# Applying two layernorms of a four-stage transformer kernel on ScalarE instead of VectorE and GpSimd

## What is computed

```python
def _layernorm(x, axis=-1, eps=1e-05):
    m = jnp.mean(x, axis=axis, keepdims=True)
    v = jnp.var(x, axis=axis, keepdims=True)
    return (x - m) / jnp.sqrt(v + eps)
...
    x = _layernorm(x + _L0_attn_ref(x, ...), axis=-1)
    x = _layernorm(x + _L0_ffn_ref(x, ...), axis=-1)     # 32 experts, 6 per token, and a shared one
    x = _layernorm(x + _L1_attn_ref(x, ...), axis=-1)
    x = _layernorm(x + _L1_ffn_ref(x, ...), axis=-1)     # gate/up/down, 384 hidden features
```

## Time and profile before

| | us |
|---|---|
| median of 3 runs | 1186.25 (1186.06 to 1188.51) |
| profiled execution, its own time | 1185.4 |
| span of its trace | 1183.6 |
| TensorE busy | 1059.0 (89%) |
| VectorE busy | 822.5 (69%) |
| ScalarE busy | 763.7 (65%) |
| GpSimd busy | 442.6 (37%) |

### The profile page before, as it was taken

One profiled execution on the slowest core, in us unless ns is written; L12 is line 12 of the kernel. 1 busy time (PEld: TensorE's weight loads), 2 busy tenths in 40 slices (PEclk: granted clock), 3 DMA queues, 4 the chain that ended last, 5 costly groups with the idle time before them and its releaser, 6 DMA issues. The chain is left out here.

```text
span 1183.6 us, 21086 instructions
## 1 busy us (share of the span) xinstructions
PE 1059.0 (89%) x5936; PEld 500.8 (42%) x5936; DVE 822.5 (69%) x1933; ACT 763.7 (65%) x983; POOL 442.6 (37%) x457
## 2 busy tenths in 40 slices
PE   3999999999999965999999999977999999999694
PEld 1122222222222224777778777832333333322573
DVE  4879998999999627887778777846444544422487
ACT  1067777777777873555555555546888888899352
POOL 0312413313211115666667656643333223300264
PEclk9999999999999986999999999978999999999898
DMA  5453222122120001434332443133331233210001
GB/s 162 130 183 95 78 65 94 50 77 81 50 94 15 2 1 34 137 120 133 114 95 92 142 120 114 62 121 107 108 93 62 59 106 106 67 39 2 1 27 45
DMA packets 74073, 97.11 MB, mean 82 GB/s; under 512 B 12700, under 2 KB 42268, under 8 KB 73628
## 3 DMA queue, kind: packets, MB, share of 16 engines
q1 hardware_dynamic: 74024, 96.51, 26.4%
HBM read 68.29 MB, written 27.79 MB: 81 GB/s over the span
## 5 line engine op out<-in xcount | busy, mean ns | idle before, releaser
L577 DVE TENSOR_REDUCE a_nmax<-a_ps_f 128x1 f32<-128x512 f32 x512 | 322.5, 684 | 41.0 <-PE a_ps_f L445 37.5
L390 ACT ACTIVATE a_prob<-a_ps_s 128x1024 f32<-128x1024 f32 x256 | 252.4, 1025 | 77.0 <-PE a_ps_s L505 75.3
L924 ACT ACTIVATE a_prob<-a_ps_s 128x1024 f32<-128x1024 f32 x256 | 249.2, 1033 | 45.4 <-PE a_ps_s L978 42.7
L1763 POOL TENSOR_TENSOR moe_hl<-moe_hid,moe_hh 128x512 fp32r<-128x512 f32 x136 | 176.1, 1299 | 112.3 <-ACT moe_hh L1657 112.2
L445 PE MATMUL a_ps_f<-a_ks,a_qs 48*128 48x512 bf16 x512 | 176.9, 414 | 28.6 <-DMA a_ks<-parts_k 10.3
L1647 ACT ACTIVATE moe_ps<-moe_ps 128x512 f32<-128x512 f32 x128 | 74.5, 582 | 118.2 <-PE moe_ps L1579 117.3
L991 PE MATMUL a_ps_o<-a_prob,a_va 128*32 128x512 f32 x1024 | 138.1, 612 | 2.4 <-ACT a_osb L912 1.3
L518 PE MATMUL a_ps_o<-a_prob,a_va 128*32 128x512 f32 x1024 | 138.0, 612 | 0.3
L445 PEld LDWEIGHTS a_ps_f<-a_ks,a_qs 48*128 48x128 bf16 x512 | 40.2, 94 | 231.2 <-DVE a_nmax L577 190.8
L505 PE MATMUL a_ps_s<-a_qs,a_ks 51*128 51x512 bf16 x512 | 135.1, 387 | 3.2 <-ACT a_prob L390 2.8
L1695 DVE TENSOR_TENSOR moe_prod<-moe_cw,moe_ps 128x512 f32<-128x512 f32 x128 | 87.5, 683 | 61.2 <-PE moe_ps L1579 52.8
(11 more groups left out here) (229 smaller groups left out, 1575.8 us busy)
## 6 DMA issues: line engine op xcount, KB each, us to landing
moe_cw<-r_weights SPq DMA_DIRECT2D x256, 128.0 KB, 2.9
parts_q<-a_parts SPq DMA_DIRECT2D x48, 256.0 KB, 2.5
parts_k<-a_parts SPq DMA_DIRECT2D x48, 256.0 KB, 2.5
a_qs<-parts_q SPq DMA_DIRECT2D x128, 96.0 KB, 2.3
a_ks<-parts_k SPq DMA_DIRECT2D x128, 96.0 KB, 2.4
a_xt<-in_x_t SPq DMA_DIRECT2D x8, 256.0 KB, 2.9
out_x<-g_X SPq DMA_DIRECT2D x8, 256.0 KB, 2.3
moe_wg<-in_wg SPq DMA_DIRECT2D x1, 1088.0 KB, 5.2
```

Of the source, the lines that this page charges most:

```text
L390: nc.scalar.activation(prob[:, u % PSLOTS, :, :], ps_s[:, u % 2, :, :], ACT.Exp, scale=float(P) ** -0.5).then_inc(exp_done, 1)
L577: nc.vector.tensor_reduce(nmax[:, half_no, h % 2, col:col + 1], ps_f[:, bank, :], AX.X, ALU.max, negate=True).then_inc(max_done, 1)
L924: nc.scalar.activation(prob[:, u % PSLOTS, :, :], ps_s[:, u % 2, :, :], ACT.Sigmoid, scale=float(HD) ** -0.5).then_inc(exp_done, 1)
L1763: nc.gpsimd.tensor_tensor(hl[:, part_at(j), :], hid[:, hid_at(j), :], hh[:, part_at(j), :], ALU.subtract).then_inc(hl_done, 1)
```

## The change

The apply of both feed-forward stages moves to ScalarE, as `Identity` with a scale and a bias per token: x * rstd + (-mean * rstd). GpSimd computes that bias in two more small operations right behind `rstd`. The experts' last block stays with GpSimd, with its semaphore count adjusted. Line numbers behind the first edit are 2, then 19 to 21 higher than before.

```diff
@@ layernorm_buffers
-            "rstd": sb("rstd", [P, NT]), "gate": sb("gate", [P, 1]),
+            "rstd": sb("rstd", [P, NT]), "minus": sb("minus", [P, NT]), "bias": sb("shift", [P, NT]),
+            "gate": sb("gate", [P, 1]),
@@ layernorm_apply_pool
-    pool.wait_ge(ln["centred"], b + 1)
+    pool.wait_ge(ln["centred"], 2 * b + 1)
@@
+def layernorm_bias(nc, pool, g, ln, b):
+
+    zero = g["zero"][:, :].broadcast_to([P, NT])
+    nc.gpsimd.tensor_tensor(ln["minus"][:, :], zero, ln["mv"][:, :, 0], ALU.subtract).then_inc(ln["centred"], 1)
+    pool.wait_ge(ln["pool"], 2 * b + 2)
+    pool.wait_ge(ln["centred"], 2 * b + 1)
+    nc.gpsimd.tensor_tensor(ln["bias"][:, :], ln["minus"][:, :], ln["rstd"][:, :], ALU.mult).then_inc(ln["centred"], 1)
+
+
+def layernorm_apply_act(nc, act, g, ln, b, y):
+
+    act.wait_ge(ln["centred"], 2 * b + 2)
+    for k in range(NT):
+        ins = nc.scalar.activation(g["X"][:, b, k, :], y[:, k, :], ACT.Identity, scale=ln["rstd"][:, k:k + 1],
+                                   bias=ln["bias"][:, k:k + 1])
+    ins.then_inc(ln["x_done"], 1)
@@ feed_forward, ScalarE's step
                     head.scalar(act, head_at(b, j))
+                if end_of(b, j, 3) is not None:
+                    layernorm_apply_act(nc, act, g, ln, end_of(b, j, 3), y)
                 if end_of(b, j) is not None:
@@ feed_forward, VectorE's step
-                if end_of(b, j, 3) is not None and not routed:
-                    layernorm_apply(nc, dve, g, ln, end_of(b, j, 3), y)
@@ feed_forward, GpSimd's step
                     layernorm_pool(nc, pool, g, ln, end_of(b, j, 2))
-                if end_of(b, j, 3) is not None and routed:
-                    layernorm_apply_pool(nc, pool, g, ln, end_of(b, j, 3), y)
+                    layernorm_bias(nc, pool, g, ln, end_of(b, j, 2))
```

## The result

The kernel became slower, by more than forecast:

| | before | after |
|---|---|---|
| median of the runs side by side | 1186.15 us (4 runs) | 1231.52 us (4 runs) |
| ratio of the medians, 95% interval | | 1.0382 (1.0357 to 1.0406) |
| profiled execution: time, span | 1185.4, 1183.6 us | 1229.75, 1227.9 us |
| granted clock over the span | 0.970 | 0.956 |

A forecast was written before the change was run, and what follows sets the result against it. It took the experts as bound by TensorE, the last stage by TensorE's 6.7 us a block plus VectorE's apply. 18.7 + 7 + 5.6 = 31.3 on 1185.4 gave 1216.7, stated as 1217 us, range 1199 to 1229.

The forecast's parts named there:

- The wait and its loop: Last stage: ScalarE's apply waits 3.2 us for GpSimd's bias, holding up copy, Silu and high part, in a loop each block.
- The break-even rival: Whole kernel: ScalarE's wait costs what VectorE's stretched apply did, 1186 us; chance 0.01.
- The turn without the clock: Last stage: one block's loop takes 10.5 us in place of 8.06; with the last two layernorms +18.7 us.
- TensorE's clock: Last stage: the clock falls after idle times of 3.8 us; 1 us for each of 7 blocks, +7 us.
- stays low: Rival, last stage: the clock stays low throughout, 3.5 us for each of 7 blocks, 1234 us; chance 0.06.
- The experts: Experts: `hl` reaches TensorE 1.0 us late; 0.8 us for each of 7 blocks, +5.6 us.
- VectorE gains nothing: Both stages: VectorE loses eight applies of 1.1 to 3.1 us from its busy time, and that gains nothing.
- the bias is there in time: Rival, last stage: activations find their bias ready, turns fall to TensorE's 6.7 us, 1181 us; chance 0.04.
- The cheap loop: Rival: the wait stands, but an activation takes 0.30 us and the clock stays up, 1200 us; chance 0.13.

The follow-up runs named there:

- e1: Changed kernel with ScalarE's apply moved to the end of its step, behind the copy, the Silu and the high part: 1191.65 us, 1.0048 to the kernel before.
- e4: Changed kernel with 16 unused 512-column matmuls added on TensorE in each of five last-stage blocks, where it waits for the copy: 1219.47 us, ratio 1.0283.
- e5: Kernel before with the two new small buffers of each layernorm's set laid out and never used: 1189.09 us, ratio 1.0030.
- e9: e8 with GpSimd's old order in the last stage, `hl` ahead of the bias: 1181.41 us, ratio 0.9958 to the kernel before.
- e8: Changed kernel with experts as before; last stage: new buffers, apply behind the high part, bias ahead of `hl`, last two blocks on VectorE: 1178.73 us.
- e6: Changed kernel with GpSimd's `ve`, `rstd` and bias operations ahead of `hl` in the last stage: 1214.10 us, ratio 1.0233 to the kernel before.
- e7: Changed kernel with the apply's activations as plain copies, without scale and bias: 1212.72 us, ratio 1.0221 to the kernel before.
- e2: Changed kernel with the change in the last stage only, the experts normalised on GpSimd as before: 1224.58 us, ratio 1.0326 to the kernel before.

## Why the prediction failed in its size

Point by point, against the profiled executions (44.35 us in all, 31.3 forecast):

- **The wait and its loop: right.** Place, length (3.2 forecast, 3.25), what waits behind it, and TensorE's idle time (3.8 forecast, 3.94) are in the trace. e1 shows that it is the place that costs: 40 of 45 us go with the apply's move alone. The break-even rival needed a turn of 8.1 us; even with a full clock it takes 10.8 (e4).
- **The turn without the clock: 10.5 forecast, 10.8 measured (e4).** Of the 0.3, 0.12 us are the activation, taken as 0.45 and measured at 0.479, four times; the rest is 0.1 each in GpSimd's chain (3.17 us from `hl` to the apply, 3.06 in the sum) and in TensorE's part (4.26 for 4.18). The six turns and the end make 1.9 us, and the last stage at full clock is about 77.2 us where the sum has 75.3: this term was +20.6, not +18.7.
- **TensorE's clock: +7 forecast, some 14 measured. This is the step that failed.** The prediction took 1 us of at most 3.5 a block, because "part of the slow time falls on work off the path". The trace shows the reverse. The clock is at 0.50 from the end of the idle time on, and what TensorE does first then is exactly what the block waits for: 11 of the 15 matmuls of the path, and the turns, run at the low level, and the clock comes up in the twelfth. The last three and the work off the path find it up again. That "the clock comes back in between" was right, but nearly all of the path has then run. The measured cost is 2.7 us a turn (e4).
- **The range.** The working gives the clock up to 3.5 us a block, and that bound alone, with the other terms as they are, is the 1234 us of the "stays low" rival. The range stops at 1229, so it left the step's own bound out. Of the 13 us by which the sum falls short, 6.8 are the clock, 5.0 the experts and 1.9 the turn; the part ahead of the experts gave 0.7 back.
- **"Stays low" as a rival** had the full price and was given 0.06, since the clock does recover in each block. It recovers, and most of the price is paid in a full turn all the same: 2.7 us of 3.5. The two cases were not the alternatives they were made to be.
- **The experts: +5.6 forecast, +10.6 measured.** By the trace 1.36 us a block are the late high and low part, forecast 1.0 at that matmul and 0.8 after what TensorE takes back; TensorE takes nothing back. Of the seven blocks only six pay; in the last TensorE does not wait. Another 0.28 a block comes from the buffers' placement (e5), which no view of the trace of before could show. Together 1.64 of the measured 1.7 a block; six such blocks and 0.26 in the last make 10.6.
- **"VectorE gains nothing": right for this placement only.** Its busy time fell by 14.3 us and no distance between adds became shorter. The rival "the bias is there in time" could not come about in this order, as the prediction says. Its mechanism is real, though: once the apply stands behind the high part (e1, e9) the last stage runs at 7.1 us a turn, and with the bias early at 6.6 (e8), the rival's 6.7.
- **The cheap loop** is refuted twice over: the activation is 0.479 us and the clock does not stay up.

Open: why the placement of the buffers behind the two small ones makes TensorE's matmuls start 0.002 us later each; what besides its length decides whether an idle time brings the clock down (e6, e7); and whether a shared port is what stretches the routing's operations in e1. None was tried by itself.

## What to carry to other kernels

A wait in an in-order queue costs what stands behind it, so place an operation by when its latest input is ready, not by where its result is wanted: with the change in the last stage alone, the activations cost 39 us in one place (e2) and gave 5 in another, further down the same step, with the last two blocks left on VectorE (e9). When a change lets TensorE idle periodically, let the range reach to the price of the full path behind the idle time, since here the slow matmuls were the first ones after it, and those were what the block waited for. And where small buffers are added, run the kernel before with the buffers alone, since the placement can be a term of its own.

## What was not expected of the hardware

- The granted clock had fallen by the end of four idle times of 3.93 to 3.94 us and was full again about 5.8 us after them (1169.05 to 1174.9); 16 matmuls without use, 3.79 us of work, kept it at 1.00 and made the kernel 12 us faster.
- The same idle time of TensorE stood before either clock: 3.21 us before 1.00 and before 0.50 (e7), 2.45 before 1.00 and before 0.52 (e6).
- Two small buffers in each layernorm's set, 16 bytes per partition each and never written, made the experts' matmuls start 0.234 us apart in place of 0.232, and the experts' blocks 0.7% longer.
- A VectorE operation of the routing that starts inside GpSimd's `hl` on 128x512 ends just behind it: a copy of 128x24 took 0.72 us, with 0.17 where no GpSimd operation stood beside it. The four TENSOR_SCALAR of the apply took 3.07 us beside GpSimd and 1.12 without.
